# An attention and mixture-of-experts block: two raw weight buffers a set, the routing weights written ahead of the indexed stores, and the burst of pairs one dense round earlier

## The reference, cut to what matters

```
scores = sigmoid(x @ gate_w.T)            # route: 4 of 8 groups, then 8 experts a token
rw     = 2.5 * chosen scores / their sum  # (tokens, 64), eight entries a row are not 0
expert_out[e] = (silu(x @ Wg[e].T) * (x @ Wu[e].T)) @ Wd[e].T      # Wg, Wu: 88 x 128
out    = sum over e of rw[:, e] * expert_out[e] + shared(x)
x      = x + layernorm(out)
```

## Time and profile before

| what | value |
| --- | --- |
| median of 3 runs | 496.69 us (495.16 to 499.41) |
| profiled execution, its own time | 497.04 us |
| its span, first to last instruction | 495.3 us |
| mean granted TensorE clock | 0.915 |
| TensorE busy with matmuls | 403.5 us (81%) |
| VectorE, ScalarE, GpSimd busy | 289.2, 213.3, 184.1 us |

### The profile page before, as it was taken

The page is one execution under the profiler, slowest core; times in us unless marked ns, Lnnn a source line. Parts: engine busy times, 40 slices in busy tenths (PEclk is TensorE's granted clock), DMA queues, the critical chain, the costliest instruction groups (busy, mean ns, idle before and its releaser), DMA issues.

```text
span 495.3 us, 7318 instructions
## 1 busy us (share of the span) xinstructions
PE 403.5 (81%) x2024; PEld 304.3 (61%) x2024; DVE 289.2 (58%) x761; ACT 213.3 (43%) x557; POOL 184.1 (37%) x242
## 2 busy tenths in 40 slices
PE   6889888297631339999969999999994999999985
PEld 5779754153421226666638999999862655555564
DVE  6667876344120126776734666665471888888885
ACT  4769963032110113332325666666533344444533
POOL 7664563657777720000000000000065566767201
PEclk9999988569757668999989999999999799999999
DMA  6088000111141427678144666665322222222211
GB/s 183 16 342 338 1 1 6 38 32 37 54 132 50 130 74 244 186 142 143 48 118 123 181 175 177 171 190 164 109 65 63 74 74 83 82 82 79 60 54 42
DMA packets 65467, 54.03 MB, mean 109 GB/s; under 512 B 7013, under 2 KB 61333, under 8 KB 65429
## 3 DMA queue, kind: packets, MB, share of 16 engines
q1 hardware_dynamic: 60469, 44.85, 31.0%
q0 software_dynamic: 4096, 8.40, 5.8%
q10 hardware_dynamic: 864, 0.33, 0.3%
HBM read 31.53 MB, written 22.02 MB: 108 GB/s over the span
## 4 chain that ended last, share of the span: by engine, by line
PE 45%; another core or an unknown queue 25%; DVE 10%; issue 9%; SPq 4%; ACT 2%; POOL 2%; DMA 1%; POOLq 0%; DVEq 0%; ACTq 0%
PE ps L1762 9%; PE ps L1935 8%; PE ps L1960 6%; PE ps L1733 5%; PE ps L1735 5%; PE ps L1734 5%; SPq L578 4%; PE ps L1913 3%; PE ps L1947 3%; DVE up_w L1295 3%; DVE hid L1305 2%; DVE picked L1409 1%; ACT picked L1082 1%; POOL xn L802 1%
## 5 line engine op out<-in xcount | busy, mean ns | idle before, releaser
L1733 PE MATMUL ps<-x_hi,w_hi 128*128 128x512 f32 (+1 forms) x184 | 101.5, 552 | 53.6 <-issue 37.4
L741 POOL DMA_INDIRECT picked<-pair_y,slots x64 | 62.4, 974 | 202.7 <-DMA pair_y<-pair_out 184.2
L991 ACT ACTIVATE ps<-ps 128x512 f32<-128x512 f32 (+1 forms) x92 | 51.7, 563 | 115.9 <-PE ps L1735 97.5
L1295 DVE TENSOR_TENSOR up_w<-ps,route_w 128x512 f32<-128x512 f32 (+1 forms) x92 | 61.1, 664 | 69.1 <-PE ps L1735 30.4
L1762 PE MATMUL ps<-hid,w_raw 128*128 128x512 f32 (+1 forms) x182 | 94.1, 600 | 1.4 <-DVE hid L1305 1.4
L1733 PEld LDWEIGHTS ps<-x_hi,w_hi 128*128 128x128 f32 x184 | 36.8, 200 | 89.0 <-issue 64.3
L1735 PE MATMUL ps<-x_hi,w_lo 128*128 128x512 f32 (+1 forms) x184 | 74.2, 403 | 0.0
L1734 PE MATMUL ps<-x_lo,w_hi 128*128 128x512 f32 (+1 forms) x184 | 74.1, 403 | 0.0
L732 POOL DMA_INDIRECT pair_x<-x_rows,slots x64 | 62.3, 973 | 21.9 <-issue 18.8
L1305 DVE TENSOR_TENSOR hid<-ps,up_w 128x512 f32<-128x512 f32 (+1 forms) x92 | 61.5, 668 | 6.2 <-ACT ps L991 2.3
L1935 PE MATMUL ps<-gu_w,pair_xt 128*128 x256 | 49.4, 315 | 0.0
(11 more groups left out here) (221 smaller groups left out, 592.8 us busy)
## 6 DMA issues: line engine op xcount, KB each, us to landing
w_raw<-in_w_experts SPq DMA_DIRECT2D x44, 192.0 KB
pair_x<-zero SPq DMA_DIRECT2D x16, 512.0 KB, 5.6
pair_in<-pair_x SPq DMA_DIRECT2D x32, 256.0 KB, 3.0
pair_y<-pair_out SPq DMA_DIRECT2D x64, 128.0 KB, 2.2
gu_w<-in_w_experts SPq DMA_DIRECT2D x22, 256.0 KB
down_w<-in_w_experts SPq DMA_DIRECT2D x16, 176.0 KB
pair_x<-x_rows,slots POOLq DMA_INDIRECT x64
picked<-pair_y,slots POOLq DMA_INDIRECT x64
```

The source lines that it names most:

```text
L741: g.indirect_dma_start(picked[:, t % 3, k, :], None, pair_y, bass.IndirectOffsetOnAxis(ap=slots[:, t, k:k + 1], axis=0)).then_inc(s_pick[t ...
L991: a.activation(bank, bank, ACT.Silu).then_inc(s_gated, 1)
L1295: v.tensor_tensor(up_w[:, k % 2, 0:w], ps[:, gate_bank(k) + 1, 0:w], route_w[:, group, 512 * dense_at(q) + lo:512 * dense_at(q) + lo + w], ...
L1733: t_.matmul(out_, hi, mhi, start=start, stop=False)
```

## The change

Four things change together.

1. `w_raw` has eight buffers instead of four, two for each set. The weights of rounds 0 and 1 are loaded at the start, and from then on a load waits for the down product of two rounds before. ScalarE and VectorE split one set further ahead (3 instead of 2). `y_t` shrinks from four to two quads, and the buffers of the burst share their room with those of the gathers.
2. In the first phase all shared steps come first (0 to 7), then the routed steps of quad 2 (8 to 11) and of quad 3 (12 to 15).
3. GpSimd writes both quads' routing weights after only four of the 64 stores, and the other 60 stores follow in one row. The stages of VectorE and TensorE are reordered to suit.
4. The burst follows dense round 3 instead of round 4. The eighth combine moves from the last round into the rounds.

```diff
-    BURST_AFTER = 4
+    BURST_AFTER = 3
-        y_t = sb("y_t", [P, QUADS, 512])
+        y_t = sb("y_t", [P, 2, 512])
-        w_raw = sb("w_raw", [P, SETS, 3 * P])
+        w_raw = sb("w_raw", [P, 2 * SETS, 3 * P])
 PE_ORDER
-  "E1 T34 F1 T35 C31 T36 Z0 T37 C32 C33 Z1 D0 E2 F2 D1 Z2 X0 E3 F3 Z3 D2 X1 Z4 D3 X2 "
-  "Z5 G2 D4 X3 N20 D5 N21 Z6 Z7 D6 Z8 D7 Z9 D8 Z10 D9 Z11 D10 G3 D11 N30 N31 Z12 Z13 "
+  "E1 T34 F1 T35 C31 T36 Z0 T37 C32 C33 Z1 D0 E2 F2 D1 Z2 X0 E3 F3 Z3 X1 D2 Z4 X2 D3 "
+  "Z5 G2 D4 Z6 X3 N20 D5 N21 Z7 Z8 D6 G3 Z9 D7 Z10 D8 N30 D9 N31 Z11 Z12 D10 Z13 D11 "
   "Z14 D12 Z15 D13 "
 ACT_ORDER
-  "... R3 Z4 O1 Z5 G2 N20 N21 Z6 Z7 Z8 Z9 Z10 Z11 G3 N30 N31 Z12 R4 Z13 Z14 R5 Z15 "
+  "... R3 Z4 O1 Z5 G2 Z6 N20 N21 Z7 Z8 G3 Z9 Z10 N30 N31 Z11 Z12 Z13 R4 Z14 R5 Z15 R6 "
 DVE_ORDER
-  "... Z2 J2 Y1 Z3 I2 O2 M2 Y2 F3 G2 H3 Z4 Y3 Z5 J3 Z6 Z7 I3 O3 M3 Z8 Z9 Z10 G3 Z11 Z12 R4 Z13 Z14 R5 Z15 "
+  "... Z2 J2 F3 Y1 Z3 H3 I2 O2 M2 Y2 J3 Z4 G2 Y3 Z5 I3 O3 M3 Z6 Z7 Z8 G3 Z9 Z10 Z11 Z12 Z13 R4 Z14 R5 Z15 R6 "
 POOL_ORDER
-  "X3 F2 M1 E2 J2 R3 E3 I0 I1 M2 F3 I2 I3 J3 I4 I5 I6 M3 " + I7 ... I31
+  "X3 F2 M1 E2 J2 R3 E3 F3 I0 M2 J3 I1 M3 " + I2 ... I31
-        FIRST = [(q, c, False) for q in SPARSE for c in range(SHARED)]
-        for q in DENSE:
-            FIRST += [(q, c, False) for c in range(SHARED)]
-            FIRST += [(q, c, True) for c in range(SETS)]
+        FIRST = [(q, c, False) for q in range(QUADS) for c in range(SHARED)]
+        FIRST += [(q, c, True) for q in DENSE for c in range(SETS)]
-        AHEAD = 2
+        def raw_of(r, c):
+            return (r * SETS + c) % (2 * SETS)
-        COMBINE_AT = {(BURST_AFTER + 1) * PER_ROUND + 7 + 5 * t: t for t in range(ST - 1)}
+        COMBINE_AT = {(BURST_AFTER + 1) * PER_ROUND + 7 + 5 * t: t for t in range(ST)}
 SyncE
-            for c in range(SETS):
-                sp.dma_start(w_raw[:, c, :], w_experts[0, c]).then_inc(s_wl[c], 16)
+            for n in range(2 * SETS):
+                sp.dma_start(w_raw[:, n, :], w_experts[n // SETS, n % SETS]).then_inc(s_wl[n], 16)
-            def reload(r, c):
-                n = (r - 1) * SETS + c
-                sp.wait_ge(s_whi, n + 1)
-                wait_w_lo(sp, n)
-                sp.wait_ge(s_down, last_user(n) + 1)
+            def reload(n):
+                old = n - 2 * SETS
+                sp.wait_ge(s_whi, old + 1)
+                wait_w_lo(sp, old)
+                sp.wait_ge(s_down, last_user(old) + 1)
 ScalarE and VectorE, in the rounds
-                    split_hi(r * SETS + k // 2 + AHEAD)
+                    split_hi(r * SETS + 3 + k // 2)
-                    split_lo(r * SETS + k // 2 + AHEAD)
+                    split_lo(r * SETS + 3 + k // 2)
 the last round
-  ACT "Z0 Z1 R2 K7 Z2 Z3 R3 Z4 ... "       DVE "Z0 Z1 R2 Z2 K7 Z3 R3 V7 Z4 C0 ... "
+  ACT "Z0 Z1 R3 Z2 Z3 Z4 ... "             DVE "Z0 Z1 R3 Z2 Z3 Z4 C0 ... "
```

More of the change, by code:

```diff
@@ L281, in build @@
         s_rw = sem("route_w_ready")
-        s_wl = [sem(f"expert_w_loaded{k}") for k in range(SETS)]
+        s_wl = [sem(f"expert_w_loaded{k}") for k in range(2 * SETS)]
         s_shl = sem("shared_w_loaded")
@@ L387, in build @@
             "B0 S1 P1 S2 P2 S3 D0 K0 P3 X0 R0 D1 R1 R2 F0 X1 L0 L1 E0 J0 D2 M0 F1 X2 J1 E1 D3 "
-            "X3 F2 M1 E2 J2 R3 E3 I0 I1 M2 F3 I2 I3 J3 I4 I5 I6 M3 "
-            + " ".join(f"I{n}" for n in range(7, 32))
+            "X3 F2 M1 E2 J2 R3 E3 F3 I0 M2 J3 I1 M3 "
+            + " ".join(f"I{n}" for n in range(2, 32))
         )
@@ L612, in load_pairs @@
                              ).then_inc(s_pin[g % 4], 16)
-            def reload(r, c):
-                n = (r - 1) * SETS + c
-                sp.wait_ge(s_whi, n + 1)
-                wait_w_lo(sp, n)
-                sp.wait_ge(s_down, last_user(n) + 1)
[L620 to L635, removed]
-                        sp.wait_ge(s_down, last_user(0) + 1)
-                        sp.wait_ge(s_slots, ST)
-                    load_late(3)
+            def reload(n):
[3 more added lines that the diff above has]
+                sp.wait_ge(s_down, last_user(old) + 1)
+                sp.dma_start(w_raw[:, n % (2 * SETS), :], w_experts[n // SETS, n % SETS]
+                             ).then_inc(s_wl[n % (2 * SETS)], 16)
+            BEFORE = (BURST_AFTER + 3) * SETS
+            for n in range(2 * SETS, BEFORE):
+                if n == BEFORE - 1:
+                    load_late(len(late))
+                    for t in range(ST):
+                        sp.wait_ge(s_scat[t], 16 * CHOSEN)
+                    for g in range(4):
+                        load_pairs(g)
+                reload(n)
+                if n == 2 * SETS:
+                    sp.wait_ge(s_fill, 16 * (PAIR_TILES // 8))
+                    sp.wait_ge(s_rw, SETS * len(DENSE))
+                    sp.wait_ge(s_tab, 1)
+                    sp.wait_ge(s_ysh, 2)
+                    sp.wait_ge(s_slots, ST)
+                load_late(3)
             load_pairs(4)
@@ L646, in _ @@
                              pair_out[:, u % 4]).then_inc(s_ps[u % 4], 16)
-            for r in range(BURST_AFTER + 2, ROUNDS):
-                for c in range(SETS):
-                    reload(r, c)
+            for n in range(BEFORE, ROUNDS * SETS):
+                reload(n)
             for t in range(ST):
@@ L1370, in split_lo @@
                 dve.wait_ge(s_up, ups_through(last_user(n - SETS)))
-                tt(w_lo[:, c, :], w_raw[:, c, 0:WD], w_hi[:, c, :],
+                tt(w_lo[:, c, :], w_raw[:, n % (2 * SETS), 0:WD], w_hi[:, c, :],
                    ALU.subtract).then_inc(s_wlo, 1)
@@ L1518, in _ @@
                 elif what == "C":
-                    dve.wait_ge(s_wl[SETS - 1], 16 * ROUNDS)
-                    rows = w_raw[:, SETS - 1, WD:WD + P]
+                    load = (ROUNDS * SETS - 1) % (2 * SETS)
+                    dve.wait_ge(s_wl[load], 16 * len(range(load, ROUNDS * SETS, 2 * SETS)))
+                    rows = w_raw[:, load, WD:WD + P]
                     link(v.bn_stats(wc_stats[:], rows))
@@ L1970, in dense_down @@
                     k = (s - STEPS0) % PER_ROUND
-                    down(s, quad_of(k), w_raw[:, k // 2, :], P)
+                    down(s, quad_of(k), w_raw[:, raw_of((s - STEPS0) // PER_ROUND, k // 2), :], P)
             def burst(lagged):
@@ L2025, in _ @@
                             pe.wait_ge(s_po, BURST)
-                        down(LAST_S + kd, q, w_raw[:, c, :], P, start=(lo > 0 and c == 0),
+                        down(LAST_S + kd, q, w_raw[:, raw_of(ROUNDS - 1, c), :], P, start=(lo > 0 and c == 0),
                              stop=(c == SETS - (2 if lo else 1)), lo=lo, w=w)
```

31 lines of the change are left out of this document (18 added, 13 removed), and 8 rows, old and new, of tables (ACT_ORDER, DVE_ORDER).

## The result

Measured beside each other, 12 runs each, the changed kernel takes 502.43 us (501.01 to 503.36) and the kernel before 498.38 us (495.16 to 499.99): a ratio of 1.0088, with a 95% interval of 1.0067 to 1.0109. That is a small loss, 4 us, inside the 1% that the prediction called the same. The profiled execution has a span of 501.0 us against 495.3, at a mean granted clock of 0.908 against 0.915.

A forecast was written before the change was run, and what follows sets the result against it. TensorE's work bounds the kernel outside the hole; inside, a long row of indexed DMAs delays its signals. Terms -1.5 - 1.5 + 5.4 + 1.2 - 1.3 = +2.3 us on 497.04 gave 499.3, median 499.0; range 484 to 508.

The forecast's parts named there:

- the hole: TensorE's idle stretch beside the stores, about 131 to 186 us before the change: four gaps, 39.1 us together.
- some 20 us a step: Inside the hole, once signals are late: each TensorE step takes 20.3 to 22.4 us instead of 2.25.
- 14 us of grace: In the row of stores: TensorE's signals become late about 14 us after the row starts, so from about 113.5.
- Row's end: GpSimd's row of 60 stores was to end at 175.5 us against 176.98: -1.5 us.
- Fewer steps ahead of the hole: Unbroken row starts earlier, 3 steps fewer before the hole, 0.6 more in it: +5.4 us, bounds -2.2 to +7.8.
- raw buffers: Two a set: 0 inside the hole, -1.5 us in the five steps behind it, 0 in steady rounds.
- Burst one round earlier: At the burst's start: a wait for `down_w` or the pairs of 0 to +4 us, taken as +1.2.
- Eighth combine: Moved out of the last round, it removes the 1.33 us wait for `w_lo` there: -1.3 us.
- the loads as the brake: Rival: waits for raw weights make the hole, so eight loaded sets give 480 to 487 us; chance 0.27.
- VectorE did not hold up the stores: Denies a rival: more VectorE work beside the 60 stores ends the row 6 us later, 505 us; chance 0.06.
- The long row bites fully: Rival, stretch 99 to 182 us: over three steps lost (+7.8), burst waits for `down_w`, about 506 us; chance 0.24.

The follow-up runs named there:

- E1: E6 with its 60 stores cut into rows of six, each row waiting until TensorE's steps have gone four further: 450.12 us, ratio to before 0.9048.
- E3: Changed kernel with all 64 indexed stores as plain GpSimd DMAs of the same bytes to consecutive rows, output wrong: 437.19 us, ratio to before 0.8752.
- E4: Changed kernel with the 64 stores issued by SyncE as plain DMAs of the same bytes, output wrong: 442.26 us, ratio to before 0.8854.
- P3: Kernel before with eight raw buffers, two a set, and the split further ahead, old orders and burst place kept: 497.76 us, ratio 0.9969.
- P2: Kernel before with the new orders and shared steps first, four raw buffers, burst after round 4, eighth combine in the last round: 507.51 us, ratio 1.0177.
- P1: Kernel before with one line changed, the burst after dense round 3 instead of 4: 497.87 us, ratio 0.9977.
- E6: Changed kernel with the burst after dense round 4 again and the eighth combine in the last round: 503.43 us, ratio to before 1.0100.
- E2: Kernel before with its row of 50 stores cut into rows of six, old order and four raw buffers kept: 478.18 us, ratio 0.9580.
- E7: E6 with its stores in rows of ten, one row for each 6.67 TensorE steps: 461.47 us, ratio to before 0.9247.

## Why the prediction was right, and where its terms were off

The cause was named rightly: E1, E3 and E4 show that the long row of indexed DMAs alone makes the hole. Of the rule behind it, the second half held, some 20 us a step once the signals are late: the up products of Z11 to Z14 were taken later one by one (2.7, 14, 31 and 40 us), ScalarE's gates at 127.53, 147.13 and 169.53, 19.6 and 22.4 us apart (forecast 20.3 to 22.4). The first half, 14 us of grace, isn't a fixed time. In the kernel before, the last signal in time ended 13.5 us after the row's start, and D12, the first that I called late, 17.6 us after it. In the changed kernel a signal that ended 11.5 us after the start was 1.2 us late, but the first long gap began at 125.45, 24 us after it, and not at about 115. TensorE was at Z17 at 187.24, as foreseen. The forecast for the whole, +2.3 us, was measured as +4.1 by the medians and +5.7 in the profiled executions. Term by term:

- *Row's end, forecast -1.5:* +0.1. It ended at 177.09 and not 175.5, since the first store came at 86.20 (forecast 82.3) and the second routing weight at 100.27. My walk through VectorE's new order was too quick.
- *Fewer steps ahead of the hole, +5.4, and raw buffers, -1.5:* +6.2 together with the row's end, against +2.4. Z21 starts at 197.80 where Z24 did at 198.74, that is 2.6 steps, against the 2.4 forecast. So the largest term came out in its net, but not in its parts, and that is luck. I had 3 steps fewer ahead of the hole and 0.6 more in it. Measured, one fewer was issued ahead of the first long gap (up to Z13, before it up to Z14), and the other 1.6 were lost in the hole: Z14 to Z16 in the 61.8 us up to Z17, against Z15 to Z18 in the 54.5 us up to Z19. The kernel before let two steps through at its first gap, because ScalarE had both gates at hand when its cast was done. What failed is what I set against this term, the two times -1.5: P3 measures the buffers at -1.5 on the old order, but P2 shows the new order at +8.8 without them, beyond my upper bound of +6.3 for order and row's end together. I priced the buffers as if the order didn't matter to them; P2's cast, which waits 38.33 us for its load, is the wait that I left out.
- *Burst one round earlier, +1.2:* 0. The gap is 3.74 against 3.71, P1 says -1.1 with an interval that includes 0. No row here shows the 8 us of a `down_w` load that I took the term from.
- *Eighth combine, -1.3:* borne out. No wait for `w_lo` in the last round, and the stretch behind the burst is 1.9 shorter than eight more steps make it.
- *Not forecast, +1.4:* the burst's first 12 us had a granted clock of 0.72 and not 0.86. P2, P3 and E6, with the burst at its old place, begin it with the same slower transpose (0.66 us against 0.41), so the burst's new place doesn't make it; E1, with the orders and the buffers, begins it with 0.41. It belongs to no part of the change.

Of the rivals, the loads as the brake fell for this change with P3, which took the loads' waits away and kept 38.4 us of gaps; E2 shows that they stand next in line. The Trainium skill, page "Trainium Kernel Development and Optimization", section "Best Practices", advises double buffers. That is right of the mechanism, as E2 shows, and worth 1.5 us of 498 in P3, as long as the row stands. VectorE did not hold up the stores: they took 966 ns on average, against 973, and 973 in E1, where VectorE was busy for 59.5 of the 100 us beside them. So what the Trainium skill, page "SBUF — State Buffer", section "SBUF: two separate sides", says of GpSimd's descriptors and VectorE's two-port mode shows no effect in these traces; no run here tells whether VectorE used that mode. "The long row bites fully" is nearest to P2, with its 507.5, and by P2 against E6 it is the change's own buffers that kept it from there.

What my text didn't ask is what the change would be worth with the cause removed. The same orders and buffers that lose 4 us beside a row of 60 are part of a kernel that is 10% faster than before.

## What to carry to other kernels

When several engines see one engine's results late while nothing is queued before them, compare the end of the producing instruction with the start of each consumer and look for what runs throughout: here one loop of DMAs on an engine that isn't in the chain at all. Such a row may be harmless in its own cost (GpSimd was never the bound) and still set the end, so pace it by the consumer's steps, in rows of four to six, and not by what its own engine can issue. And price two edits to the same stall together: two buffers were worth 1.5 us in one order and some 4 in the other, where a load came to end last, and much of a change's worth can be hidden behind a stall that it doesn't touch.

## What the runs showed of the hardware

- Indexed DMAs of GpSimd, 64 KB each and one every 1.26 us, in a row without a pause, let TensorE's signals reach ScalarE, VectorE and SyncE late. The first ones are late by 1 to 3 us and end 7 to 12 us after the row's start (E7, changed kernel); in the row of 60 the delay grew to 40 us (Z14's up product, 138.4 to 177.99), with the signals of one step taken 8.46 us apart, and 14 us after the row's end (from 191.36) the steps were 2.25 us again. Signals of VectorE to TensorE stayed in time.
- The same bytes as plain DMAs of GpSimd take 544 ns each and delay nothing in 31 us. Rows of six indexed ones with pauses of 0.8 to 5.3 us cost TensorE 1.8 us at most at a time, and that behind the pauses of 0.8; after a row of six or ten the signals were in time again within 4.6 us (E1 at 163.29, E7 at 180.97).
- What joins an indexed DMA on GpSimd to the signals of TensorE, and whether their number, their time or the number of signals beside them counts, stays open: all rows here have the same pace.
